# Reader-less matmuls in TensorE's waits between the last attention block and the first expert

## The reference

```python
x = x + tanh(g_xattn) * attention(layernorm(x), ctx)     # 4096 tokens, 16 heads, 128 context rows
x = x + tanh(g_ffn) * moe(layernorm(x))                  # 8 experts, top 2, capacity 1280 rows each

# moe: 
logits = clip(xf @ router_w.T); top_v, top_i = top_k(logits, 2)
slot = expert * C + position of the token in that expert's queue     # kept if position < C
xb = rows gathered into [E, C, D]
h = silu(xb @ w_gate.T) * (xb @ w_up.T);  yb = h @ w3.T
out[token] += yb[slot] * weight
```

## Time and profile before

| | |
|---|---|
| three timed runs | 2752.97 us median, 2751.85 to 2756.25 |
| span of the profiled execution | 2753.4 us (no other time is given for it) |
| mean granted TensorE clock | 0.983 of full speed |
| TensorE busy | 2662.1 us, 97% of the span |
| first block ends | about 575.5 us |
| first matmul of an expert | 591.40 us |

### The profile page before, as it was taken

The page is one execution under the profiler, slowest core; times in us unless marked ns, Lnnn a source line. Parts: engine busy times, 40 slices in busy tenths (PEclk is TensorE's granted clock), DMA queues, the critical chain, the costliest instruction groups (busy, mean ns, idle before and its releaser), DMA issues.

```text
span 2753.4 us, 41258 instructions
## 1 busy us (share of the span) xinstructions
PE 2662.1 (97%) x14422; PEld 2396.4 (87%) x14423; DVE 1397.1 (51%) x2725; ACT 980.9 (36%) x2543; POOL 420.6 (15%) x395
## 2 busy tenths in 40 slices
PE   6999999959999999999999999999999999999988
PEld 4888888859999888888888888888888999989987
DVE  5787777734444444444444444454444444445555
ACT  4766666522223322232222322232222322232343
POOL 4445455420000100010000200010000200020030
PEclk8999999969999999999999999999999999999999
DMA  7522222232112310132110421131100510133242
GB/s 263 202 79 83 78 94 80 88 117 85 46 46 51 91 46 23 46 71 75 46 36 32 84 86 53 61 70 65 46 33 36 121 46 29 39 79 123 76 125 80
DMA packets 60035, 208.40 MB, mean 76 GB/s; under 512 B 9564, under 2 KB 9836, under 8 KB 51602
## 3 DMA queue, kind: packets, MB, share of 16 engines
q1 hardware_dynamic: 43282, 175.30, 17.8%
q0 software_dynamic: 16640, 31.69, 6.0%
HBM read 145.60 MB, written 67.70 MB: 77 GB/s over the span
## 4 chain that ended last, share of the span: by engine, by line
PE 76%; issue 2%; DVE 1%; ACT 0%; DMA 0%; DVEq 0%; POOL 0%; ACTq 0%; POOLq 0%
PE bank L1549 75%; PE bank L1555 1%; DVE yacc L1489 0%; DVE slotsT_lo L1458 0%; DVE h L1509 0%; ACT slotsT_hi L1381 0%; DMA xrow<-expert_rows 0%; ACT later_hi L1377 0%; ACT yout L1405 0%; ACT h_hi L1419 0%; POOL out_dram L1363 0%; DVE w_lo L1452 0%; DVE early_lo L1452 0%; DVE later_lo L1452 0%; DVEq L1488 0%
## 5 line engine op out<-in xcount | busy, mean ns | idle before, releaser
L1509 DVE TENSOR_TENSOR h<-silu,bank 128x384 f32<-128x384 f32 (+2 forms) x320 | 183.9, 575 | 827.3 <-PE bank L1549 818.3
L1549 PE MATMUL bank<-slotsT_hi,early_hi 128*128 128x384 f32 (+2 forms) x1280 | 445.2, 348 | 13.9 <-issue 9.9
L1549 PE MATMUL bank<-slotsT_hi,w_hi 128*128 128x384 f32 (+2 forms) x1280 | 442.1, 345 | 5.1 <-DVE w_lo L1452 5.1
L1549 PE MATMUL bank<-slotsT_lo,early_hi 128*128 128x384 f32 (+2 forms) x1280 | 443.1, 346 | 0.0
L1549 PE MATMUL bank<-slotsT_hi,early_lo 128*128 128x384 f32 (+2 forms) x1280 | 442.3, 346 | 0.3 <-issue 0.3
L1549 PE MATMUL bank<-slotsT_lo,w_hi 128*128 128x384 f32 (+2 forms) x1280 | 441.8, 345 | 0.0
L1549 PE MATMUL bank<-slotsT_hi,w_lo 128*128 128x384 f32 (+2 forms) x1280 | 440.8, 344 | 0.0
L1419 ACT CAST h_hi<-h 128x384 fp32r<-128x384 f32 (+2 forms) x320 | 169.3, 529 | 741.0 <-DVE h L1509 741.0
L1413 ACT ACTIVATE silu<-bank 128x384 f32<-128x384 f32 (+2 forms) x320 | 162.5, 508 | 722.6 <-PE bank L1549 722.1
L1489 DVE TENSOR_TENSOR yacc<-bank,yacc 128x512 f32<-128x512 f32 x464 | 316.6, 688 | 167.6 <-PE bank L1549 167.6
L1549 PE MATMUL bank<-later_hi,h_hi 128*128 128x512 f32 x1008 | 399.7, 397 | 0.3 <-DVE yacc L1489 0.3
(11 more groups left out here) (212 smaller groups left out, 3908.9 us busy)
## 6 DMA issues: line engine op xcount, KB each, us to landing
staged<-in_moe_w_dram SPq DMA_DIRECT2D x33, 1536.0 KB
raw<-in_moe_w_dram SPq DMA_DIRECT2D x32, 1536.0 KB
xrow<-expert_rows SPq DMA_DIRECT2D x42, 520.0 KB, 9.0
expert_rows<-zeros SPq DMA_DIRECT2D x40, 520.0 KB, 7.7
xin<-in_x_dram SPq DMA_DIRECT2D x17, 512.0 KB, 3.7
xres<-in_x_dram SPq DMA_DIRECT2D x15, 512.0 KB, 3.7
out_dram<-xres SPq DMA_DIRECT2D x15, 512.0 KB
staged<-in_L_xattn_Wq_dram SPq DMA_DIRECT2D x1, 1024.0 KB, 10.6
```

What stands on the lines that cost most here:

```text
L1509: nc.vector.tensor_tensor(h32[q % 2][:, 0:W], silu[q % 2][:, 0:W], UB[q % 2][:, 0:W], ALU.mult)\
L1549: last = nc.tensor.matmul(out_ap, st, mv, start=(at == 0), stop=(at == n - 1))
```

## The change

TensorE gets matmuls whose product nobody reads: 128x128 stationary, 512 moving columns, always `start=True, stop=True` into a PSUM bank that is free there. In the first block there are 53 of them, in the second 34.

```diff
+                    def keep_warm(n):
+                        for i in range(n):
+                            nc.tensor.matmul(bank[7][:, :], wq_hi[:, i % KD, 0:P], wo_hi[:, i % KD, :], start=True, stop=True)
+
                     def turn_rows(blk):
                         for a in range(2):
+                            if is_last(blk):
+                                keep_warm((4, 8)[a])
 
                             pe.wait_ge(row_ready, 2 * blk + a + 1)
...
                     router(LAST)
+                    keep_warm(8)
                     positions(LAST)
+                    keep_warm(5)
 
                     pe.wait_ge(sums_ready, 1)
                     nc.tensor.matmul(bank[0][:, 0:E], ones[:, :], chosen[:, 0, :], start=True, stop=True).then_inc(counts_ready, 1)
+                    keep_warm(28)
...
+                    def keep_warm(n):
+                        for i in range(n):
+                            nc.tensor.matmul(GB[0][:, :], early_hi[:, i % KD, 0:P], early_hi[:, i % KD, :],
+                                             start=True, stop=True)
+
+                    keep_warm(14)
                     for i in range(XA):
                         if i % 2 == 0:
                             pe.wait_ge(xrow_loaded[i // 2], 16)
...
                         turn(i, xa_tp)
+                    keep_warm(20)
```

## The result

The changed kernel takes 2763.26 us, median of six runs (2761.55 to 2764.37), against 2752.97: ratio 1.0034, interval 1.0023 to 1.0045. It is 10.3 us slower, outside the range and on the side that had a chance of 0.08. Its profiled span is 2762.3 us, 8.9 more than before.

A forecast was written before the change was run, and what follows sets the result against it. TensorE, busy 97% of the span, was taken as the bound, so only an earlier start of the steady experts counts. Terms -0.8 + 0.3 - 0.2 = -0.7 us gave 2752.3 us, range 2748.7 to 2756.2.

The forecast's parts named there:

- the side that had a chance of 0.08: Whole kernel: slower than before by over 0.2%, chance 0.08.
- Other code placement changes the stalls at later experts: Later experts: listed as something that would show the forecast wrong, without a size or chance.
- The ceiling and the border: Attention's end to first experts: at most 5.4 us gain, 0.2%, about what a measurement can tell from no change.
- Last transposes, router, 8 behind, `positions`: First block before the barrier: -0.46, -0.87, +0.6 and -0.1, together -0.8 us, with ends -2.6 and +1.0.
- The router term: Last block's router: clock falls between transposes and router's end or just behind; gain 0 to 1.73, middle taken, -0.87.
- rival 4: Slot scatters: new timing shifts VectorE's splits away from the slow scatter, 2.46 us gained, total -3.2; chance 0.08.
- 28 behind `counts`: Before the barrier: 6.4 us at full clock in 9.20 us of room, covered, 0, bound +2.8.
- 14 ahead of the first rows: Second block's start: 3.2 us at full clock in 3.77 us of room, covered, 0, bound +2.2.
- rival 2: New matmuls run slow and stand in the way, the 14 delaying transposes 2.2 us: +5.6, 2758.6; chance 0.08.
- 20, branch and first expert: Behind tile 3's transposes: branch later, +0.3 (bounds -0.5, +4.1); clock lost again before first expert matmuls, -0.2.
- rival 3: Branch into expert code comes late because issue does not run ahead: +4.1 there, total +3.1, 2756.1; chance 0.10.
- Rival 1: Clock holds through router and code stall too: -5.4 us, 2747.6; chance 0.07.

The follow-up runs named there:

- (5): Kernel before with 174 instructions that never run added to TensorE's program ahead of the expert code, no new matmuls: 2761.37 us, ratio 1.0038.
- (6): Changed kernel with instructions that never run ahead of the expert code, filled to 256 added in all: 2752.45 us, ratio 1.0002 against the kernel before.
- 14: Changed kernel with 18 instructions (16 never run) ahead of the expert code, 192 added in all: 2751.96 us, ratio 0.9995 against the kernel before.
- (13): Kernel before with 174 never-run instructions behind the expert code instead of ahead of it: 2753.18 us, ratio 0.9997.
- (15): Changed kernel at 256 added instructions, with VectorE's six splits moved ahead of the last block's routing: 2753.23 us, ratio 0.9996 against the kernel before.
- (12): Kernel before with VectorE's six splits of the first expert's weights moved ahead of the last block's routing: 2751.93 us, ratio 0.9987.
- (8): Only the second block's 34 matmuls, filled to 256 added instructions by ones that never run: 2752.74 us, ratio 1.0002 against the kernel before.
- 64: Kernel before with 64 instructions that never run ahead of the expert code: 2754.04 us, ratio 0.9992.
- 192: Kernel before with 192 instructions that never run ahead of the expert code: 2752.09 us, ratio 0.9990.
- 256: 256 instructions added in all, matmuls included, as in (2), (6) and (8); kernel before not run with 256 never-run ones; (6) measured 1.0002.
- 128: Kernel before with 128 instructions that never run ahead of the expert code: 2763.27 us, ratio 1.0026.
- 174: 174 instructions added ahead of the expert code: the changed kernel's matmuls and weight loads (1.0034), or never-run ones in the kernel before (1.0038).
- (1): Kernel before with 174 executed semaphore increments on TensorE behind the counts matmul, no new matmuls: 2782.48 us, ratio 1.0109.
- (2): Changed kernel with 82 executed semaphore increments on TensorE, 256 added instructions in all: 2762.55 us, ratio 1.0038 against the kernel before, runs 2754.09 to 2764.92.

## Why the prediction was wrong

**The step that failed** is the one that costed the 174 instructions only by when they run, in "What the new matmuls cost and what they hide behind" and in the "Sum": every term stands between 547 and 596 us, and behind that the sum has nothing. "Other code placement changes the stalls at later experts" was named among what would make it wrong, and had no price and no chance of its own. It was nearly the whole result: 9.3 of the 10.3 us by itself (5), none when undone in the changed kernel (6, 14), none for size without place (13). The profile before already had the means for a bound: branches from 0.35 to 4.8 us long in the same loop (TensorE's branch records), and a 2.33 us gap of code at an expert. Two returns to the dispatch that turn from the short kind to the long one are up to 8 us of branch.

**The ceiling and the border.** That a success would lie "on that border" of what can be told was right: with a neutral place the change measures 1.0002 and 0.9995. These fit the forecast of -0.7 us, and 0 just as well. No run reached the ceiling of 5.4 us, so it is untested.

**Last transposes, router, 8 behind, `positions`.** Right in mechanism. The clock did fall once more around the router, in every profile that has the first block's matmuls. In the profile after it came as late as it could help (-2.0 us in all, forecast -0.8); in (6) and (15) it came at the router, and the last `positions` was 0.4 us late in both, inside the ends -2.6 and +1.0. The router term was 1.63 us instead of the middle, 0.87.

**The scatters.** Not in the sum, and what came was the opposite of rival 4. Sooner `counts` let the splits start first: +1.08 us. That freeing them would bring 2.46 us was right as a size: (12) gave 2.45.

**28 behind `counts`.** Right: 6.60 us at the full level, 4.32 us of wait left.

**14 ahead of the first rows.** Wrong, and rival 2 had this part of it. The 28 end at 568.7, the barrier comes at 573.0, and that pause of 4.3 us loses the clock: 5.05 us instead of 3.2, first transposes +1.38. I had taken a pause of 1 to 3 us. The 28 ended about 1 us sooner than forecast, as `positions` had come sooner, and the caught scatter kept the barrier from following. (6) shows the same with 4.30 us; (8), which has no 28, doesn't bear on it.

**20, branch and first expert.** The size is near, the sign was wrong: from the first transposes to the first expert matmul it is 12.13 us before and 11.83 after, -0.30 (the -0.52 and +0.22 of the table) where +0.3 was forecast, inside the ends. The branch into the expert's code begins 35.35 us behind the common event before and 36.02 after, when the 20 still have 2.3 us to run, so issue was some 10 matmuls of 0.23 us ahead and not 17. The pause of 4.03 us came as forecast, and rival 3 (+4.1) is excluded. The clock was still at 1.00 for the first matmuls of the expert and fell under them, 0.62 us gained instead of 0.2.

**Rival 1** (the clock holds through) did not come in any profile.

**What stays open.** Why 64, 192 and 256 are good and 128 and 174 bad. The runs give six points with 0, the packets ahead of the branch tell the two kinds apart, and why that packet is missing at 128 and 174, although the hint is given, isn't shown. Expert 0 and expert 5 branch back from the same code; whether it is the target or the branch that must lie well was not told apart. The third gap (3.19 us, 3.30 in (1), 3.02 in (5)), which comes with 174 and not in the profile of 128, has no branch at its place; one instruction packet moves in it. The 10.8 us between the runs of (2) are not explained: only its fastest was profiled. (6), the same kernel with padding that never runs, has ten runs from 2747.36 to 2755.48.

## What to carry to other kernels

When a change adds or removes instructions ahead of a loop of long, branching code, its time contains the new place of that code, here up to 9 us, more than the 5.4 us that this change could win at best by its ceiling. Measure it against a copy of the old kernel with as many instructions that never run, and try a few other amounts, before you believe either a gain or a loss. The matmuls that were to hold the clock left pauses of some 4 us in front of the next real work, the clock fell again, and they gained nothing that can be measured. Moving six vector instructions away from an indirect DMA brought the second block 2.45 us forward.

## What the runs showed of the hardware that was not expected

- A branch back to the same instruction took 0.35 us or about 4 us, by the amount of code ahead of both: 0.35 to 0.38 at +0, +64, +192, +256; 3.94 to 4.84 at +128 and +174. All the short ones had an instruction packet in the 15 us ahead of them, none of the long ones had.
- The clock can fall after a pause and not in it: 1.00 was granted in all of the 4.3 and the 4.0 idle us of the changed kernel, and 0.65 on average in the work that followed (the windows above). It also fell in a pause: 0.53 over 3.33 idle us before, and 0.86 over 4.11 in (15), from 585.00 to 589.11.
- A semaphore increment as an instruction of its own cost 0.15 us on TensorE, 26 us for 174.
- An indirect DMA beside fp32 splits took 0.97 us when it began 0.18 us ahead of them, 4.50 when it began 0.03 behind; the caught ones ended 0.85 us behind the last split.
